# An attention and experts kernel whose second load of scores' operands is issued later, in nine transfers

## The reference

```python
qkv = x @ w_qkv                                  # (4, 512, 3 * 256)
q, k, v = ...                                    # each (4, 512, 16 heads, 16)
scores = einsum('bqhd,bkhd->bhqk', q / 4, k)     # causal mask
out = einsum('bhqk,bkhd->bqhd', softmax(scores), v) @ w_out
x = layernorm(x + out)
w = the four largest of softmax(x @ gate) for each token, scaled to sum to 1
y[t] = sum over its four experts e of w[t, e] * (u * silu(g)) @ down_proj[e],  g, u = split(x[t] @ gate_up_proj[e])
x = layernorm(x + y)
```

## Time and profile before

| | us |
|---|---|
| three runs, median (lowest to highest) | 448.34 (447.44 to 452.43) |
| the profiled execution, its own time | 452.55 |
| its span, from the first to the last instruction | 450.6 |
| TensorE matmuls busy | 397.5 |
| VectorE busy | 293.4 |
| ScalarE busy | 238.8 |
| GpSimd busy | 236.4 |
| DMA, moved in the span | 72.68 MB, 161 GB/s |

### The profile page before, as it was taken

How to read it: one execution, slowest core, us unless ns; L and a number is a source line. 1 busy time by engine, 2 the same in 40 slices (tenths; PEclk the granted TensorE clock), 3 DMA queues, 4 the chain that set the end, 5 groups by cost and what they waited for, 6 DMA issues and landing times.

```text
span 450.6 us, 10602 instructions
## 1 busy us (share of the span) xinstructions
PE 397.5 (88%) x3045; PEld 241.0 (53%) x3045; DVE 293.4 (65%) x891; ACT 238.8 (53%) x522; POOL 236.4 (52%) x373
## 2 busy tenths in 40 slices
PE   5876799999998789997898989997999999987991
PEld 3532465555565445744455456664767767654560
DVE  1233683778548997599979939873565666543564
ACT  2521164666554568655675736654565656545142
POOL 4421132433233348662686373777777776646662
PEclk9999799999999999999999999999999999999796
DMA  5556433253645416548554753564665655339772
GB/s 167 164 161 180 140 108 109 79 157 96 186 128 162 141 38 208 180 144 225 158 164 138 220 150 95 162 193 144 182 191 153 170 156 167 110 76 375 276 303 93
DMA packets 53367, 72.68 MB, mean 161 GB/s; under 512 B 10163, under 2 KB 45629, under 8 KB 51777
## 3 DMA queue, kind: packets, MB, share of 16 engines
q1 hardware_dynamic: 46128, 54.83, 43.0%
q0 software_dynamic: 6912, 16.93, 10.1%
q10 hardware_dynamic: 272, 0.26, 0.2%
HBM read 44.24 MB, written 29.66 MB: 164 GB/s over the span
## 4 chain that ended last, share of the span: by engine, by line
PE 40%; SPq 20%; DVE 16%; issue 10%; POOL 6%; DMA 4%; ACT 2%; ACTq 0%; DVEq 0%; POOLq 0%
SPq L488 13%; PE PS L799 6%; PE PS L756 5%; DVE MX L1353 5%; POOL scratch_slots L1692 4%; PE PS L778 4%; PE PS L727 4%; SPq L470 3%; PE PS L653 3%; PE PS L739 2%; DMA scratch_qk<-PA 2%; PE PS L938 2%; DVE MX L1355 2%; PE PS L760 2%; PE PS L931 2%
## 5 line engine op out<-in xcount | busy, mean ns | idle before, releaser
L1069 ACT ACTIVATE PT<-PS 128x512 f32<-128x512 f32 x160 | 93.0, 596 | 52.4 <-PE PS L778 47.5
L1353 DVE TENSOR_REDUCE MX<-PS 128x1 f32<-128x384 f32 (+1 forms) x192 | 88.7, 503 | 29.4 <-PE PS L760 29.0
L1701 POOL DMA_INDIRECT scratch_y<-Y,XG x80 | 79.5, 994 | 36.0 <-issue 18.0
L1673 POOL TENSOR_SCALAR_AFFINE_SELECT PT<-PT 128x256 f32<-128x256 f32 (+1 forms) x140 | 50.7, 370 | 82.8 <-ACT PT L1069 80.8
L1692 POOL DMA_INDIRECT scratch_slots<-XP,RI x64 | 64.4, 1006 | 38.1 <-DVE XP L1287 18.5
L756 PE MATMUL PS<-KS,QS 96*128 96x512 bf16 (+3 forms) x256 | 62.4, 305 | 20.9 <-DVE MX L1355 10.1
L653 PE MATMUL PS<-W,XGT 128*64 x320 | 61.9, 337 | 0.9 <-DVE WG L1208 0.7
L778 PE MATMUL PS<-QS,KS 98*128 98x512 bf16 (+3 forms) x256 | 60.9, 299 | 1.3 <-ACT PT L1069 1.1
L655 PE MATMUL PS<-WG,XGT 128*64 128x192 f32 x320 | 61.9, 337 | 0.0
L756 PEld LDWEIGHTS PS<-KS,QS 96*128 96x128 bf16 x256 | 21.7, 100 | 50.7 <-DVE MX L1353 25.6
L653 PEld LDWEIGHTS PS<-W,XGT 128*64 128x64 f32 x320 | 41.2, 139 | 13.4 <-issue 8.6
(11 more groups left out here) (233 smaller groups left out, 685.6 us busy)
## 6 DMA issues: line engine op xcount, KB each, us to landing
XG<-scratch_slots SPq DMA_DIRECT2D x160, 65.0 KB, 2.6
scratch_qk<-PA SPq DMA_DIRECT2D x48, 128.0 KB
QS<-scratch_qk SPq DMA_DIRECT2D x48, 128.0 KB, 2.7
KS<-scratch_qk SPq DMA_DIRECT2D x48, 128.0 KB, 2.7
W<-_L_ffn_gate_up_proj_dram SPq DMA_DIRECT2D x16, 288.0 KB
YL<-scratch_y SPq DMA_DIRECT2D x8, 512.0 KB, 6.5
W<-in_L_ffn_down_proj_dram SPq DMA_DIRECT2D x8, 288.0 KB
scratch_slots<-pad SPq DMA_DIRECT2D x17, 130.0 KB, 3.3
```

Source lines behind the costliest of these rows:

```text
L1069: e.activation(PT[:, p % NPT, n, :], PS[:, 2 + (rank[u] - 1) % 2, :], ACT.Exp).then_inc(st_exp, 1)
L1353: t = e.tensor_reduce(M[:, h, qt:qt + 1], PS[:, kk, c0:c0 + w], AX.X, ALU.max)
L1673: e.affine_select(out=d, in_=d, compare_op=ALU.is_ge, fill=0.0, base=0, pattern=[[0, 1 if n < 2 else 2], [1, 128]], channel_multiplier=-1) ...
L1701: e.indirect_dma_start(out=YK[:, :], out_offset=bass.IndirectOffsetOnAxis(ap=XG[:, j % NXG, D + 1:D + 2].bitcast(I32), axis=0), in_=Y[:, j ...
```

## The change

There are three edits.

1. In `make_plan()` the projection of key block (1, 2) moves up beside that of query block (1, 0), ahead of the first scores. The rest of the two chains is queued into slots 0 to 2, so that the residue of (1, 0) follows `max(0, 0)`. `load(1)` is queued for slot 4, behind the stores of (1, 2); it stood behind the stores of (1, 0).
2. A load takes four transfers for QS and five for KS. The order of the six products within the 96 partitions changes so that query part 0 fills the partitions 0, 2 and 4 of each six (one transfer of 48 rows, each source row being read three times), and key part 1 the partitions 0 and 3 (one transfer of 32 rows). The products and the bytes are the same. `ld_in` counts to 144.
3. `keep_busy` ahead of the first scores has 6 matmuls in place of 14.

```diff
-TERMS = ((0, 0), (1, 0), (2, 0), (0, 1), (1, 1), (0, 2))
+QS_ROWS = ((0, 2, 3, 0), (1, 6, 1, 1), (3, 6, 1, 1), (5, 6, 1, 2))
+KS_ROWS = ((0, 3, 2, 1), (1, 6, 1, 0), (2, 6, 1, 0), (5, 6, 1, 0), (4, 6, 1, 2))
...
             if b == 1:
-                plan += [(kind, b, 0) for kind in ("qk", "resid", "part", "qkout")]
-                plan += [("load", 1), ("qk", b, 2)]
-                put(0, ("resid", b, 2))
-                put(1, ("part", b, 2))
-                put(2, ("qkout", b, 2))
+                plan += [("qk", b, 0), ("qk", b, 2)]
+                put(0, ("resid", b, 0))
+                put(1, ("part", b, 0), ("qkout", b, 0), ("resid", b, 2))
+                put(2, ("part", b, 2), ("qkout", b, 2))
+                put(4, ("load", 1))
...
-                    for t, (q, _) in enumerate(TERMS):
-                        e.dma_start(QS[r][t:96:6, :, :], SC[0, b, half, q].rearrange("d h t -> d (h t)")).then_inc(ld_in[r], 16)
+                    for t, step, n, part in QS_ROWS:
+                        e.dma_start(QS[r][t:96:step, :, :],
+                                    SC[0, b, half, part].rearrange("d h t -> d (h t)").unsqueeze(1)
+                                    .broadcast_to([HD, n, 8 * S])).then_inc(ld_in[r], 16)
...
-                    for t, (_, k) in enumerate(TERMS):
-                        e.dma_start(KS[r][t:96:6, :, :], SC[1, b, half, k].rearrange("d h t -> d (h t)")).then_inc(ld_in[r], 16)
+                    for t, step, n, part in KS_ROWS:
+                        e.dma_start(KS[r][t:96:step, :, :],
+                                    SC[1, b, half, part].rearrange("d h t -> d (h t)").unsqueeze(1)
+                                    .broadcast_to([HD, n, 8 * S])).then_inc(ld_in[r], 16)
...
                     if (i, n) == (0, 0):
-                        keep_busy(14)
+                        keep_busy(6)
...
-                    e.wait_ge(ld_in[r], 192 * (g // RG + 1))
+                    e.wait_ge(ld_in[r], 144 * (g // RG + 1))
```

## The result

The changed kernel takes 446.0 us (median of 20 runs, 442.42 to 450.44) where the kernel before takes 449.14 (20 runs, 445.94 to 453.03). The ratio is 0.9914, with a 95% interval of 0.9888 to 0.9940: 3.9 us faster, where 7.4 were forecast. The ratio is taken over the fast runs of each kernel alone (those within 1.5% of its fastest), so it is not the ratio of the two medians. The profiled execution of the changed kernel took 445.82 us (span 444.0).

A forecast was written before the change was run, and what follows sets the result against it. It took SyncE's queue, which stalls TensorE ahead of pair 4, as the bound. A gain of 8.3 us up to pair 4 less 0.9 for X gave 7.4 us, from the median of 448.34 to 440.9 us; range 437.5 to 445.5.

The forecast's parts named there:

- the old stall: TensorE's 6.36 us wait before 47.72 us, traced through VectorE and ScalarE to stores queued behind load(1); forecast to go.
- rival (d): Steady part: the gain is lost again to something that does not move; 446.5 us with three quarters lost, chance 0.09.
- step 3: VectorE's walk to pair 4: despite a new 2.0 us wait, pair 4 starts at 48.1, not 56.36; gain 8.3 us.
- Step 1: Nine transfers a load: load(0) issues end at 21.6, 1.9 us earlier; wide ones land up to 1 us later than 2.7.
- step 2: First pair: stores 1.9 us earlier; copy of (1,0) at 26.3, of (1,2) at 28.4, first score at 26.4.
- rival (c): Loads: wide transfers run on fewer DMA engines; below four, the kernel is slower, 453 us; chance 0.04.
- Step 4: SyncE's queue behind load(1): x(2) goes out at 45.8, so TensorE waits 0.9 to 1.9 us for X; 0.9 taken.
- Step 5: Six later loads: each saves SyncE 3 x 0.63 us, worth nothing at the end; bounds plus 0.5 and minus 1.

The follow-up runs named there:

- e9: The changed kernel, unchanged, profiled a second time: 443.61 us, ratio 0.9877 to the kernel before.
- e15: The changed kernel, unchanged, profiled once more on another occasion: 445.2 us, ratio 0.9927 to the kernel before.
- e17: The changed kernel's new order alone, with twelve transfers a load and 14 unused matmuls as before, on an undisturbed chip: 448.3 us, ratio 0.9995 to the kernel before.
- e13: The changed kernel with 14 unused matmuls in place of 6 ahead of the first scores, disturbed chip: 509.96 us, ratio 0.9932 to the kernel before.
- e14: The changed kernel with 14 unused matmuls in place of 6 ahead of the first scores, undisturbed chip: 445.62 us, ratio 0.9934 to the kernel before.
- e16: The changed kernel with 13 unused matmuls in place of one ahead of max(1, 2), undisturbed chip: 443.44 us, ratio 0.9892 to the kernel before.
- e12: The changed kernel with 13 unused matmuls in place of one ahead of max(1, 2), disturbed chip: 507.4 us, ratio 0.9820 to the kernel before.
- e8: The kernel before with 28 unused matmuls in place of one ahead of max(2, 1): 450.02 us, ratio 1.0011 to the kernel before.
- e7: The changed kernel with ScalarE's copy of (1, 2) behind the part of (1, 0) and 9 unused matmuls ahead of max(1, 2): 442.37 us, ratio 0.9864.
- e19: The changed kernel with ScalarE's copy of (1, 2) behind the part of (1, 0), 9 unused matmuls ahead of max(1, 2), disturbed chip: 500.27 us, ratio 0.9863.
- e5: The changed kernel with ScalarE's copy of (1, 2) behind the part of (1, 0): 445.23 us, ratio 0.9921 to the kernel before.
- e10: The changed kernel's new order alone, with twelve transfers and 14 unused matmuls as before, disturbed chip: 510.09 us, ratio 0.9934 to the kernel before.
- e2: The changed kernel's new order alone, with twelve transfers and 14 unused matmuls as before, disturbed chip: 510.98 us, ratio 1.0068 to the kernel before.

## Why the prediction was wrong in size

The direction held, and so did the mechanism as far as the old stall goes: it is gone, and pair 4 starts earlier. From pair 4 to the end it takes 393.6 us (444.0 less 50.35) after and 394.2 (450.6 less 56.36) before, and 390.6 and 390.8 in e9 and e15, so nothing was lost later and rival (d) is out. The size did not hold: 7.4 us forecast, 3.9 measured (2.7 to 5.0), and 3.3 to 5.5 over the three measurements. Two terms failed: above all the projection in step 3, taken at 1.88 us, which took 3.57 on the path since TensorE's clock had fallen; and the landings in steps 1 and 2, taken too short. By the forecast's steps, from the first copy (0.4 us earlier in the profile after):

1. **Step 1** held for SyncE: nine issues took 5.67 us (15.54 to 21.21) against 5.7 forecast. It failed on the landings. I forecast 2.7 us, up to 1 more for the two wide transfers. All of them, the 128 KB ones too, took 4.0 to 4.2, and the third store of (0, 1), issued at 22.60, let ScalarE's copy start only at 26.90, 4.3 us later, where 3.4 had passed before (24.83 to 28.19). With twelve transfers the landings of loads were 3.0 us in e17. That nine issues press the same bytes into less time and the queue on the DMA engines grows fits this and is not shown by itself. Of the 1.9 us that step 2 takes from here, the copy of (1, 0) got 1.2: it comes 18.05 us after the first copy in the mean of the six profiles with twelve transfers, and 16.85 in that of the fourteen with nine, where 16.2 was forecast. The Trainium skill (DMA: Bandwidth & Descriptors, Why a DMA increments its semaphore by 16 and not by 1) was cited for wide transfers using all 16 engines; the runs agree, since 384 KB and 128 KB landed in 4.0 and 4.2 us, and rival (c) did not occur.
2. **Step 2**: the first score came at 25.97 (forecast 26.4). The copy of (1, 2) came 19.2 us after the first copy, 0.9 more than the forecast's 18.3: the landings above. The third edit, without which the first maximum would lie on the path, is worth 0.4 us there (e13, e14), and it costs more by the wait that it leaves to TensorE.
3. **Step 3** is the step that failed. The wait that it names came as forecast: VectorE stands 2.21 us (forecast 2.0), ScalarE 3.08. What I left out is TensorE's share: it stands 2.84 us, its granted clock falls to 1.2 GHz, and the projection of (1, 3), which I took at the 1.88 us of the earlier trace rows, took 3.57. It lies on the path, since VectorE waits 3.21 us for it, and with the clock kept 1.51 (e16): 1.7 us of head. From the copy of (1, 1) to the first exponential the forecast has 15.3 us (33.5 to 48.1, and 0.70), the profile after 17.1, and e12, where the clock is kept and GT is not waited for, 15.4. That the half clock in the old stall is contained in the gain was right: it was worth 0.8 to 1.2 us there (e8).
4. **Step 4**: `x(2)` went out at 46.40 (forecast 45.8), and TensorE did not wait for it, as it came 2.3 us later than forecast itself. Where TensorE comes earlier, or X goes out later, the wait is there: 0.29 (e16), 0.60 (e7), 0.97 (e19), 0.98 (e12), 1.41 (e14) and 1.47 us (e13). The 0.9 was a fair price for a head that was not reached. But I passed over GT, which is in the same queue between `load(1)` and X: in e17 and e5 it is what ends the gain.
5. **Step 5** held: the stretch from 50 to 414 us has the busy times of before, within 1 us for every engine.

The sum in heads: 8.3 us forecast up to pair 4 (the 7.4 and the 0.9 for X, which the head does not contain), less 1.7 for the projection, less 0.9 for the landings, less 0.4 because the profiled head before was 46.97 where two have a mean of 46.6, gives 5.3; measured are 5.4. At the end 7.4 less the same terms, with the 0.9 for X given back, is 5.3 too, and the time shows 3.9. I also took the whole gain of one profile from the median of other runs without asking how far the head itself moves between executions: 0.8 us in the kernel before, 0.4 in the one after, 2.9 in the order alone.

**What stays open.** The three ratios of the changed kernel give 3.9, 5.5 and 3.3 us, a mean of 4.2, while the heads give 5.4; no profile shows where the 1.2 us between them go. Between executions of the changed kernel the stretch from pair 4 to the end differs by 3.0 us (390.6 in e9, 393.6 in the profile after), so one pair of profiles can't find them. In the profile after and in e15 the clock is also down near 159 us (0.72 from 158 to 164), in e9 not, and it may be such places that differ from run to run. What makes the clock fall is not settled either: after 2.84, 2.96 and 2.83 us of standing it fell, after 2.69 and 2.54 too (e10, e2), after 2.55 it did not (e17), but then after 1.72. What nine transfers alone are worth at the end was not measured on an undisturbed chip.

## What to carry to other kernels

When an edit takes out a long stall, walk the new timeline for the short waits of TensorE that it leaves, and ask of each which operation stands right behind it: a projection that another engine waits for took nearly twice its time when the clock fell there (1.7 us of head), and the scores behind the old stall cost 0.8 to 1.2 us. Price the half clock from a fixed point behind the wait, since the head as a whole moves by as much between executions. Where such a wait of 2 to 3 us can't be removed, unused matmuls in it were the better cure here (1.1 to 1.7 us of head) than shifting the wait elsewhere (e5). Of a queue that is passed by a load, list every small transfer behind it with the time at which its reader now comes, and count a denser burst with longer landings, not with those of the looser one.

## What the runs showed of the hardware

- Nine transfers for the same 1.57 MB landed in 4.0 to 4.2 us each in the profile after (medians of each size; 3.3 to 4.5 in the fourteen profiles with nine), where twelve landed in 2.5 to 3.0 in six profiles. The DMA share was 0.96 and 0.88 from 36 to 40 us where it had been 0.84 and 0.55. The width of a transfer (384, 256 or 128 KB) made a difference of 0.2 us to its landing in the profile after.
- TensorE's granted clock went to 1.2 GHz after only 1.09 us of standing ahead of the router's product (e5), and after 1.72 us (e17), but stayed at 2.4 GHz after 1.71 us ahead of `max(1, 2)` (e14). A fall lasted some 3.4 us in the changed kernel and over 6 us in e17, where the clock is 0.95 from 44 to 46 us, 0.50 until 52 and 0.85 until 54.
- On three of five occasions, on two chips, every kernel took some 60 us more, with pauses of up to 9 us in the middle that no engine of the core explains.
- One issue of `load(1)` took 1.5 to 1.8 us in four profiles (before, e8, e13, e14) and 1.1 to 1.3 in three (e2, e10, e17), where the others took 0.59, and what stood behind it on the queue went out later.
